# A decoder layer's self-attention: the turn of the probabilities moves from TensorE to VectorE and a round trip through DRAM

## The reference, cut to what matters

```python
scale = q[:, ::step].reshape(b, -1)            # q = layernorm(x), step = s // 4
qk = jnp.einsum('bsd,btd->bst', q, k)
scaled_qk = qk * scale[:, None, :]
softmax_qk = jax.nn.softmax(scaled_qk, axis=-1)
return jnp.einsum('bst,btv->bsv', softmax_qk, v)
```

## Time and profile before

| | |
|---|---|
| median of 3 runs | 3876.82 us (3873.74 to 3878.27) |
| span of the profiled execution | 3891.2 us |
| TensorE busy | 3788.4 us, 97% of the span |
| VectorE busy | 2395.0 us, 62% |
| ScalarE busy | 1432.7 us, 37% |
| GpSimd busy | 1534.5 us, 39% |
| DMA | 381.89 MB, mean 98 GB/s |

### The profile page before, as it was taken

One profiled execution on the slowest core, in us unless ns is written; L12 is line 12 of the kernel. 1 busy time (PEld: TensorE's weight loads), 2 busy tenths in 40 slices (PEclk: granted clock), 3 DMA queues, 4 the chain that ended last, 5 costly groups with the idle time before them and its releaser, 6 DMA issues. The chain is left out here.

```text
span 3891.2 us, 63669 instructions
## 1 busy us (share of the span) xinstructions
PE 3788.4 (97%) x19001; PEld 2532.2 (65%) x19161; DVE 2395.0 (62%) x6222; ACT 1432.7 (37%) x1793; POOL 1534.5 (39%) x860
## 2 busy tenths in 40 slices
PE   8999999999999899999999999999999999999998
PEld 7888888888877444544444444544444777777776
DVE  6544444444458688888888788878887533433135
ACT  3111222233224455455545555445555221222332
POOL 1000000000013667766677666766665222312234
PEclk9999999999999999999999999999999999999999
DMA  4001000145555322222112222222111433328579
GB/s 157 32 32 32 32 32 32 44 172 178 191 179 186 94 57 55 57 57 46 35 38 57 58 57 58 54 57 55 33 36 49 151 126 132 114 92 278 185 263 332
DMA packets 223177, 381.89 MB, mean 98 GB/s; under 512 B 17544, under 2 KB 102056, under 8 KB 222892
## 3 DMA queue, kind: packets, MB, share of 16 engines
q1 hardware_dynamic: 192876, 301.34, 26.7%
q0 software_dynamic: 14752, 49.29, 3.5%
q10 hardware_dynamic: 15264, 27.79, 1.9%
HBM read 229.71 MB, written 148.66 MB: 97 GB/s over the span
## 5 line engine op out<-in xcount | busy, mean ns | idle before, releaser
L1103 DVE CUSTOM_DVE_ANT_0 xf_unread<-xa_mx_ps,mask_q 128x402 bf16<-128x402 f32 x1984 | 1036.0, 573 | 290.3 <-PE xa_mx_ps L1096 156.7
L1726 ACT ACTIVATE probs<-xa_scores 128x1024 f32<-128x1024 f32 (+1 forms) x416 | 417.5, 1024 | 417.0 <-PE xa_scores L1600 371.6
L1726 ACT ACTIVATE xa_probs<-xa_scores 128x1024 f32<-128x1024 f32 (+1 forms) x416 | 417.3, 1024 | 397.8 <-PE xa_scores L1600 355.1
L1561 POOL TENSOR_TENSOR xa_sums<-xa_sums,xa_probs 128x1024 f32<-128x1024 f32 x220 | 519.7, 2383 | 18.1 <-POOL xa_sums L1561 15.7
L1561 POOL TENSOR_TENSOR xa_sums<-xa_sums,probs 128x1024 f32<-128x1024 f32 x220 | 519.3, 2381 | 18.9 <-POOL xa_sums L1561 15.3
L1600 PE MATMUL xa_scores<-mask_t,ident_b 128*128 128x512 bf16 (+1 forms) x1505 | 499.7, 387 | 5.3 <-issue 0.2
L1096 PE MATMUL xa_mx_ps<-xa_kp,queries 96*128 96x402 f32 x1024 | 364.2, 418 | 0.8
L1096 PE MATMUL xa_mx_ps<-xf_kp,queries 96*128 96x402 f32 x960 | 341.5, 418 | 0.4
L1594 PE MATMUL xa_scores<-queries,xf_kp 97*128 97x512 f32 (+1 forms) x832 | 284.2, 423 | 16.3 <-ACTq L1748 8.2
L1096 PEld LDWEIGHTS xa_mx_ps<-xa_kp,queries 96*128 96x128 f32 x1024 | 181.7, 189 | 172.2 <-DVE xf_maxima L1103 111.6
L1594 PE MATMUL xa_scores<-queries,xa_kp 97*128 97x512 f32 (+1 forms) x832 | 284.7, 423 | 1.8 <-ACT probs L1726 1.8
(11 more groups left out here) (415 smaller groups left out, 7388.0 us busy)
## 6 DMA issues: line engine op xcount, KB each, us to landing
bridge_rows<-sorted_in SPq DMA_DIRECT2D x78, 256.0 KB
sorted_out<-ex_made ACTq DMA_DIRECT2D x78, 256.0 KB
queries<-qT_high SPq DMA_DIRECT2D x30, 512.0 KB
xf_kp<-kT_high SPq DMA_DIRECT2D x16, 800.5 KB, 12.4
xa_kp<-kT_high SPq DMA_DIRECT2D x16, 800.5 KB
rows<-in_ctx SPq DMA_DIRECT2D x16, 768.0 KB, 5.1
values<-cxl_v SPq DMA_DIRECT2D x48, 256.0 KB
kT_high<-cxl_kT_high SPq DMA_DIRECT2D x12, 768.0 KB, 4.0
```

The source lines that it names most:

```text
L1103: return dve.tensor_tensor_reduce(out=unread[slot % 2][:, :], in0=scores[:, 0:MKEYS], in1=mask_q[:, half * QB + qt, MFIRST[kb]:MFIRST[kb] ...
L1561: pool.tensor_tensor(sums[pr][:, :, :], left[pr][:, :, :], right[pr][:, :, :], ALU.add).then_inc(pool_added, 1)
L1726: act.activation(prob[ring][pr][0:keys, :, :], scores[pr][0:keys, :, :], ACT.Exp, scale=SCALE).then_inc(exped, 1)
```

## The change

From tile 1 on TensorE turns no probabilities. VectorE transposes them in squares of 32x32 from `prob` into `scaled` (one instruction for all 2048 columns). SP writes `scaled` to a DRAM tensor `turned_p` (1 MB), waits until it has landed, and reads it back into `prob` in four strips of 32 partitions (256 KB each), which puts the squares in their places. ScalarE makes the high part from there, and GpSimd the low part, which VectorE made before. The next exp waits until GpSimd has made the four low parts; the next tile's first scaled block waits until the write to DRAM has landed. Tile 0 keeps the way over TensorE.

On SP, each tile's load_add, store and load_norm go ahead of its `move`, and x for the norm is loaded one tile earlier. The scales of batches 1 to 3 are loaded one in each of three tiles instead of all at once. In the last tile nine of the twelve groups of turned weights go ahead of weigh(31), the other three follow its blocks 0 to 2. The store of a tile is issued behind load_add of the next. Context lines and moved brackets are cut here:

```diff
--- before.py
+++ after.py
...
+SQUARE = 32
+QB = P // SQUARE
+MOVED = 16 * QB
...
-def self_attention(nc, ident, x, k, v, x1, opening, weights, context):
+def self_attention(nc, ident, x, k, v, x1, opening, weights, context, turned_p):
...
+        prob_by_key = prob.rearrange("p j (c a k) -> p a (j c) k", a=QB, k=SQUARE)
+        squares = scaled.rearrange("p a (c q) -> p a c q", q=SQUARE)
+        raw_pT = prob.rearrange("p i (c q) -> p c i q", q=SQUARE)
...
-        pT_ps = [ps(f"pT_ps{i}", [P, KB, P]) for i in range(2)]
+        k_ps = [ps(f"k_ps{i}", [P, KB, P])[:, :, :] for i in range(2)]
...
-        k_ps = [pT_ps[0][:, :, :], pT_ps[1][:, :, :], o_ps[:, :].rearrange("p (c n) -> p c n", n=P)]
+        first_ps = list(k_ps)
+        k_ps.append(o_ps[:, :].rearrange("p (c n) -> p c n", n=P))
...
+        p_out, p_in = sem("p_out"), sem("p_in")
...
+        def wait_moved(eng, t):
+            eng.wait_ge(p_in, MOVED * t)
+
...
+        AHEAD = GROUPS_W - FULL
...
                 def load_scale(b):
...
+
+                def move(t):
+                    sp.wait_ge(p_turned, t)
+                    sp.dma_start(turned_p, scaled).then_inc(p_out, 16)
+                    sp.wait_ge(p_out, 16 * t)
+                    for a in range(QB):
+                        sp.dma_start(prob[a * SQUARE:(a + 1) * SQUARE, :, :],
+                                     turned_p[:, a, :].rearrange("(i k) n -> k i n", k=SQUARE)).then_inc(p_in, 16)
...
-                for b in range(1, B):
-                    load_scale(b)
-                store(0)
-                with sp.Fori(0, tiles - 3) as t:
+                load_scale(1)
+                for t in range(2):
+                    if t > 0:
+                        load_add(t)
+                        store(t - 1)
...
-                    load_add(t + 1)
+                    move(t + 1)
+                    load_scale(t + 2)
+                with sp.Fori(0, tiles - 5) as t:
+                    load_add(t + 2)
...
+                    load_norm(t + 5)
+                    move(t + 3)
...
-                for t in (tiles - 2, tiles - 1):
+                for t in (tiles - 3, tiles - 2, tiles - 1):
...
-                    if t == tiles - 1:
-                        sp.wait_ge(exped, tiles + 2)
-                        sp.dma_start(opening.rows[:, 0, 0:FULL, :],
-                                     context[0][0:FULL * P, :].rearrange("(r p) n -> p r n", p=P)).then_inc(rows_in, 16)
-                        sp.wait_ge(p_turned, NB * tiles + NB + 1)
-                        sp.dma_start(opening.rows[:, 1, 0:FULL, :],
-                                     context[0][FULL * P:2 * FULL * P, :].rearrange("(r p) n -> p r n", p=P)).then_inc(next_rows_in, 16)
-                    store(t)
+                    store(t - 1)
+                    if t < tiles - 1:
+                        move(t + 1)
+                sp.wait_ge(p_out, 16 * (tiles - 1))
+                sp.dma_start(opening.rows[:, 0, 0:FULL, :],
+                             context[0][0:FULL * P, :].rearrange("(r p) n -> p r n", p=P)).then_inc(rows_in, 16)
+                sp.wait_ge(pT_low, NB * tiles + NB)
+                sp.dma_start(opening.rows[:, 1, 0:FULL, :],
+                             context[0][FULL * P:2 * FULL * P, :].rearrange("(r p) n -> p r n", p=P)).then_inc(next_rows_in, 16)
+                store(tiles - 1)
...
                 def scale_step(b):
...
+
+                def low_p(t):
+                    for j in range(NB):
+                        mine = slice(j * KB, (j + 1) * KB)
+                        pool.wait_ge(pT_high, NB * t + j + 1)
+                        pool.tensor_tensor(pT[1][:, mine, :].rearrange("p c (i q) -> p c i q", q=SQUARE), raw_pT[:, mine, :, :],
+                                           words(pT[0][:, mine, :]).rearrange("p c (i q) -> p c i q", q=SQUARE),
+                                           ALU.subtract).then_inc(pT_low, 1)
...
-                step(2)
-                for b in range(1, B):
-                    step(b + 2)
-                    scale_step(b)
-                with pool.Fori(0, tiles - B - 2) as t:
-                    step(t + B + 2)
+                pool.sem_inc(pT_low, NB)
+                for t in range(B + 1):
+                    step(t + 2)
+                    if t > 0:
+                        low_p(t)
+                    if 0 < t < B:
+                        scale_step(t)
+                with pool.Fori(0, tiles - 3 - B) as t:
+                    step(t + B + 3)
+                    low_p(t + B + 1)
+                low_p(tiles - 2)
+                low_p(tiles - 1)
...
-                def turn_p(t, j):
+                def turn_first_p(j):
...
-                        pe.wait_ge(exped, t + 3)
-                    pe.wait_ge(pT_low, NB * t + j + 2)
+                        pe.wait_ge(exped, 3)
+                    if j >= len(first_ps):
+                        pe.wait_ge(pT_low, NB + j - len(first_ps) + 1)
...
-                        last = pe.transpose(pT_ps[j % 2][:, n, :], prob[:, j, n * P:(n + 1) * P], ident[:, :])
-                    last.then_inc(p_turned, 1)
+                        last = pe.transpose(first_ps[j % 2][:, n, :], prob[:, j, n * P:(n + 1) * P], ident[:, :])
+                    last.then_inc(k_turned, 1)
...
                 def weigh(t, j):
...
-                    pe.wait_ge(pT_low, NB * t + j + 4)
+                    pe.wait_ge(pT_low, NB * (t + 1) + j + 1)
...
                 def tile(t, ahead):
-                    if ahead >= 1:
-                        for j in range(NB - 1):
-                            score(t + 1, j)
-                    turn_p(t, 0)
-                    turn_p(t, 1)
-                    if ahead >= 1:
-                        score(t + 1, NB - 1)
+                    first = isinstance(t, int) and t == 0
+                    for j in range(NB) if ahead >= 1 else ():
+                        if first and j == NB - 1:
+                            turn_first_p(0)
+                            turn_first_p(1)
+                        score(t + 1, j)
...
+                    for n in range(AHEAD) if ahead == 0 else ():
+                        turn_last(n)
...
-                        if j + 2 < NB:
-                            turn_p(t, j + 2)
-                        for n in range(FULL) if ahead == 0 else ():
-                            turn_last(FULL * j + n)
-                    for n in range(FULL * NB, LAST_GROUPS) if ahead == 0 else ():
+                        if first and j + 2 < NB:
+                            turn_first_p(j + 2)
+                        if ahead == 0 and AHEAD + j < GROUPS_W:
+                            turn_last(AHEAD + j)
+                    for n in range(GROUPS_W, LAST_GROUPS) if ahead == 0 else ():
...
-                pe.sem_inc(p_turned, NB + 1)
...
                 def exp(t):
-                    act.wait_ge(p_turned, NB * t + 1 + NB)
+                    act.wait_ge(pT_low, NB * (t + 1))
...
                 def high_p(t, j):
...
-                    act.wait_ge(p_turned, NB * t + j + 2 + NB)
-                    act.activation(pT[0][:, j * KB:(j + 1) * KB, :], pT_ps[j % 2][:, :, :], ACT.Copy).then_inc(pT_high, 1)
+                        wait_moved(act, t)
+                    mine = slice(j * KB, (j + 1) * KB)
+                    act.activation(pT[0][:, mine, :].rearrange("p c (i q) -> p c i q", q=SQUARE), raw_pT[:, mine, :, :],
+                                   ACT.Copy).then_inc(pT_high, 1)
+
+                def high_first_p(j):
+                    act.wait_ge(k_turned, T1C + j + 1)
+                    act.activation(pT[0][:, j * KB:(j + 1) * KB, :], first_ps[j % 2], ACT.Copy).then_inc(pT_high, 1)
...
                 def tile(t, ahead):
-                    high_p(t, 0)
-                    high_p(t, 1)
-                    if ahead >= 2:
+                    for n in range(AHEAD) if ahead == 0 else ():
+                        high_last(n)
+                    if isinstance(t, int) and t == 0:
+                        high_first_p(0)
+                        high_first_p(1)
...
-                    for j in (2, 3):
-                        high_p(t, j)
-                        for n in range(FULL) if ahead == 0 else ():
-                            high_last(FULL * (j - 2) + n)
-                    for n in range(2 * FULL, LAST_GROUPS) if ahead == 0 else ():
+                        high_first_p(2)
+                        high_first_p(3)
+                    else:
+                        for j in range(NB):
+                            high_p(t, j)
+                        if ahead >= 2:
+                            high_n(t + 2)
+                    for n in range(AHEAD, LAST_GROUPS) if ahead == 0 else ():
...
-                with act.Fori(0, tiles - 2) as t:
-                    tile(t, 2)
+                tile(0, 2)
+                with act.Fori(0, tiles - 3) as t:
+                    tile(t + 1, 2)
...
                 def scale_block(t, j):
```

(36 more changed lines are left out.)

## The result

The changed kernel takes 3817.1 us in the median of four runs (3816.5 to 3817.7), beside 3875.3 for the kernel before on the same chip. The ratio is 0.985 [0.983, 0.986], a saving of 58.1 us.

A forecast was written before the change was run, and what follows sets the result against it. TensorE's own work was taken to bound the self-attention loop. Removed transposes save 51.6 us, less 3.1 for the last tile and 2.2 for the clock: 46.3 off 3876.8 gives 3831 us, range 3822 to 3868.

The forecast's parts named there:

- The bound and the price of the transposes: Self-attention loop: TensorE alone sets the period; removing its probability transposes saves 1.75 us a tile, 51.6 us in all.
- The second of my two ways: Pricing a tile's 16 transposes as the remainder of TensorE's 24.39 us period after its products: 1.81 us.
- L: Length of the probabilities' round from one exp to the next, a second possible period: 21.8 us against TensorE's 22.6.
- The way out: Writing a tile's 1 MB of turned probabilities from SBUF to DRAM: 5.3 us, 4.3 to 7.8.
- The way back: Reading the 1 MB from DRAM in four strips of 32 partitions: 5.9 us, with 4.3 and 10.0 as ends.
- The turn: VectorE's transposing of a tile's probabilities in squares: 2.3 us, at most 4.6 if two passes were needed.
- the low part, 5.2: GpSimd making a tile's four low blocks at 1.30 us each: 5.2 us in the round trip.
- The margin: In the loop, TensorE keeps the bound over the probabilities' round trip with 0.8 us a tile to spare.
- rival one: The round trip sets the period, 23.6 us; total 3860, chance 0.24. Its formula: net saving 30 x (24.16 - L).
- The tail: Last tile: weigh(31) waits for the whole round trip, TensorE stands 3 to 4 us; 3.1 us lost before any clock loss.
- the clock: Lower granted clock on TensorE after its stall before weigh(31): 2.2 us lost, 0 to 2.8.
- VectorE's wait for x_norm goes, worth nothing: Loading x_norm a tile earlier removes VectorE's wait in the loop but saves nothing, since VectorE isn't the bound.

The follow-up runs named there:

- the idle turns: The changed kernel with 16 transposes of the identity a tile put back on TensorE from tile 1 on; 3879.4 us, ratio 1.001.
- The changed kernel again: The changed kernel with no edit, measured once more in a later session; 3832.1 us, ratio 0.986 to the kernel before.
- the kernel meant to test it: The changed kernel with the read back from DRAM cut into four 256 KB transfers, each into all 128 partitions; 4018.0 us, ratio 1.031.
- the second way out: The changed kernel with the 1 MB written to DRAM twice, one after the other, each waited for; 3931.8 us, ratio 1.009.
- The pads: Semaphore increments added on TensorE: 101 in the changed kernel's last tile, 3836.6 us; 155 at the start of the kernel before, 3887.4 us.

## Why the prediction was right, and where not

**The bound and the price of the transposes: right.** From the first addition to the last scores it was 720.2 us and is 666.7, 53.5 less, where the sum had 51.6 for what I took as 29.5 tiles. With the 1.59 us that TensorE stood in tile 1, it is 55.1, or 1.87 a tile, and the idle turns gave 1.85. The second of my two ways, 1.81 as the remainder of the period, was the nearer one, and I took the first. The term was 3.5 us too small, and the wait in the first round, for which the sum had nothing, took 1.6 of it back. A further 1.9 us came ahead of the first addition: the stretch from 48 to 53 us had a clock of 0.68 before and 1.00 after. The changed kernel again had 0.66 there and its first addition at 61.5, so that part belongs to a single execution.

**The loop: right in its sum, with two errors that cancel.** L was worked out as 21.8 and is 21.1. The way out was 5.3 by seven stores of a later stage and is 3.8. The way back was 5.9 by a load to 128 partitions and is 6.97 in one tile and 7.35 in the next. The turn, 2.3, and the low part, 5.2, are 2.31 and 5.03. In the table of stretches the DMA engines are busy for 0.92 of the way back and move 207 GB/s, where the earlier trace rows had 401 GB/s at a share of 1.04. The Trainium skill, "SBUF — State Buffer", section "SBUF: two separate sides", Door 1, gives 32 partitions 8 of 16 ports and so spoke against the change here, with half the rate and an estimate of 6.9 us by that rule: the trace agrees. It was the better term, and the shorter way out made up for mine. That the partitions are the cause isn't shown, as the kernel meant to test it changed the number of engines as well.

**The margin: right.** Exp waits for the maximum, TensorE never waits in the loop, and a longer loop costs its excess in every tile. The formula of rival one is a little mild for the stage: 121 us where the way back in 14.07 cost it 135, and 40 (with L = 25.5, as measured) where the second way out cost it 47.5 (862.9 less 815.4). What it lacks lies in the tail, which took 50.1 and 46.6 us from the last scores, where the formula has 44.6 and 41.9. In the totals the later stages hide this: 121.6 and 35.4.

**The tail: right in kind, 0.8 us short.** The forecast was 3.1 and 2.2 for the clock, 5.3. Measured are 39.0 - 32.9 = 6.1. Weigh(31) starts 21.7 us after the last scores (forecast 21.1), and the idle time before it is 5.72, not 3 to 4: the groups of weights were done sooner than VectorE's pace gave. The granted clock was 0.68 and 0.64 in the two stretches from 745 to 755 us, as forecast from the two sparse stretches of the earlier trace rows.

**"VectorE's wait for x_norm goes, worth nothing": wrong as a statement, though not in the sum.** No run puts the earlier load into the kernel before, so its worth there isn't shown. In the new kernel its place ahead of `move` is what keeps the loop at TensorE's pace: behind the strips the last scores end at 788.9 instead of 727.1, 62 us later, more than the whole gain. My reason looked at VectorE's slack with the old order of its work. I hadn't asked what it costs if that cover is gone, and I priced SP's wait inside `move` at the 5 us of the way out; the larger part of it is the 14.6 us for VectorE's turn. The scales over three tiles were priced at nothing, and undoing them moved the last scores by no more than executions differ (1.0).

**The error of the total lies outside the stage.** With the marks compared, stage against stage, 53.5 - 6.1 is 47.4 beside a forecast of 46.3, and 49.3 with the 1.9 ahead of the first addition. The measured 3817.1 lies 13.4 us below the 3830.5 of the sum: 1.5 because the kernel before measured 3875.3 instead of 3876.8, 3.0 inside the stage, and 8.8 behind it. With the first two alone it would have been 3826, well inside the range. The step that failed is the last one of the sum, 3876.8 - 46.3: it takes the stage's saving as the kernel's, and so puts every later stage at nothing, without a reason. The runs showed 8.8 us in its place by the medians; in the profiles the cross-attention went from 1723.7 to 1713.5 us and the stage between gave 2.8. The pads take 5.7 us behind the stage away in one kernel and give 8 or more in the other, so TensorE's place in its program is shown to move it, and how it does so stays open. With a term of 0 to 10 us for the later stages, the range would have reached 3817. Its sign could not be had from the trace of before.

## What to carry to other kernels

A round trip that must fit beside the bounding engine is priced as one sum around the buffer that it owns; here the sum held to 0.7 us although two terms were off by over 1 us each and cancelled by luck, and every us beyond the bound's period then costs that us in every tile. When a queue's program gets a wait in the middle, ask of every load behind it how many us of lead it loses, and move it ahead of the wait: here that order was worth the whole change. Adding or removing a hundred unrolled instructions moved a later, untouched stage by 7 to 10 us in 1720 here, so a small gain is to be read from the marks of its own stage and not from the total alone.

## What the runs showed of the hardware

- VectorE turns 128x2048 values in squares of 32 in 2.31 us, as long as its maximum over the same values (2.29).
- Four transfers of 256 KB to 32 partitions each take 6.97 to 7.35 us from the first issue, at 207 GB/s with the DMA engines at 0.92. Four of the same size whose slowest dimension is 4 take 14.07, at a share of 0.26 and 98 GB/s where nothing else runs. One of 1 MB from 128 partitions to DRAM takes 3.8.
- GpSimd reads blocks in runs of 32 values at the same pace as contiguous ones: 1.30 us for 128x512, the least of the earlier trace rows. VectorE's normalizing took 1.48 instead of 0.55 us when it started beside such a block.
- Semaphore increments on TensorE start 0.15 us apart (101 of them from 745.32 to 760.78, 155 from 2.20 to 25.74), though they count as no busy time. The stage's end moved by less (11.7 and 18.5 us), as part of them fell in time in which TensorE stood anyway.
- The time of an unchanged stage depended on its place in TensorE's program: 1713.5 to 1716.6 us at 4080 and 4336 instructions, 1720.4 to 1723.7 at 4112 to 4181.
